# Splitting both halves of a score batch in one slot, and scaling keys and queries on ScalarE instead of VectorE, in a two-layer transformer kernel

## The reference

```
q = (x @ Wq + bq).reshape(b, n, 32, 128)      # k and v alike; b = 1, n = 1024
q = rmsnorm(q, gq);  k = rmsnorm(k, gk)        # over the 128 of a head
scores = einsum('bhnd,bhmd->bhnm', q, k) / sqrt(128)
attn   = softmax(scores)
out    = einsum('bhnm,bmhd->bnhd', attn, v).reshape(b, n, 4096)
return out @ Wo + bo
```

## Time and profile before

| | |
|---|---|
| median of 3 runs | 3506.22 us (3501.73 to 3507.86) |
| the profiled execution | 3506.65 us, of which 3504.5 us lie between its first and last instruction |
| busy over the span | PE 88%, DVE 61%, POOL 45%, ACT 38% |
| TensorE clock granted, mean | 0.96 of full |
| first layer (0 to 1210 us) | PE 1166.98 us busy, clock 0.99 |
| the changed attention (1280 to 3240 us) | PE 1624.39 us busy of 1960, DVE 1331.94, ACT 842.93, POOL 976.06, clock 0.94 |
| last feed-forward part (3240 to 3504 us) | PE 241.71 us busy of 264, clock 0.97 |

### The profile page before, as it was taken

How to read it: one execution, slowest core, us unless ns; L and a number is a source line. 1 busy time by engine, 2 the same in 40 slices (tenths; PEclk the granted TensorE clock), 3 DMA queues, 4 the chain that set the end, 5 groups by cost and what they waited for, 6 DMA issues and landing times. The chain is left out here.

```text
span 3504.5 us, 56557 instructions
## 1 busy us (share of the span) xinstructions
PE 3091.4 (88%) x17632; PEld 2766.9 (79%) x17632; DVE 2131.8 (61%) x3189; ACT 1334.6 (38%) x2375; POOL 1577.9 (45%) x1075
## 2 busy tenths in 40 slices
PE   8999999999999778888888888888888888886998
PEld 7999989898988567777777777777777777775786
DVE  3444444445444576667676666766666676666655
ACT  3333333333333234444444444444444444443322
POOL 3333333333333224544545554554554555444665
PEclk9999999999999999999999999999999999998999
DMA  3211111211121024444454444445444444545642
GB/s 119 59 55 58 54 58 54 59 54 59 53 59 40 22 81 154 159 152 165 153 165 149 158 157 151 161 155 167 150 154 162 149 163 155 163 144 177 179 137 60
DMA packets 311498, 413.82 MB, mean 118 GB/s; under 512 B 35968, under 2 KB 242832, under 8 KB 311312
## 3 DMA queue, kind: packets, MB, share of 16 engines
q1 hardware_dynamic: 273728, 278.05, 27.3%
q10 hardware_dynamic: 37680, 135.02, 9.6%
q0 software_dynamic: 32, 0.02, 0.0%
HBM read 259.85 MB, written 136.31 MB: 113 GB/s over the span
## 5 line engine op out<-in xcount | busy, mean ns | idle before, releaser
L1354 ACT ACTIVATE b_prob<-b_s_ps,b_shift 128x1024 f32<-128x1024 f32 x256 | 286.0, 1117 | 1017.4 <-DVE b_shift L1507 1012.6
L82 PE MATMUL b_pj_kq<-b_w_hi,xT_hi 128*128 128x384 f32 x1008 | 368.3, 365 | 8.4 <-DVE b_nat L1477 8.4
L83 PE MATMUL b_pj_kq<-b_w_lo,xT_hi 128*128 128x384 f32 x1008 | 362.0, 359 | 0.0
L84 PE MATMUL b_pj_kq<-b_w_hi,xT_lo 128*128 128x384 f32 x1008 | 358.1, 355 | 0.0
L1286 POOL TENSOR_TENSOR b_pT_lo<-b_pT_lo,b_pT_hi 128x1024 fp32r<-128x1024 f32 x128 | 303.7, 2373 | 53.1 <-ACT b_pT_hi L1343 53.1
L1286 POOL TENSOR_TENSOR pT_lo<-pT_lo,pT_hi 128x1024 fp32r<-128x1024 f32 x128 | 303.8, 2374 | 48.5 <-ACT pT_hi L1343 48.5
L1513 DVE STREAM_TRANSPOSE b_blocks<-b_prob 128x1024 f32<-128x1024 f32 x256 | 315.5, 1233 | 0.1
L82 PE MATMUL a_pj<-b_w_hi,xT_hi 128*128 128x256 f32 x1024 | 295.4, 288 | 11.9 <-DVE xT_lo L647 11.1
L82 PE MATMUL b_o_ps<-pT_hi,b_v_hi 128*128 128x256 f32 x512 | 159.4, 311 | 165.2 <-POOL pT_lo L1286 165.2
L1507 DVE TENSOR_REDUCE b_shift<-b_s_ps 128x1 f32<-128x1024 f32 x256 | 303.0, 1184 | 0.9 <-PE b_s_ps L84 0.9
L506 ACT ACTIVATE a_sig<-a_pj 128x512 f32<-128x512 f32 x192 | 115.1, 600 | 486.4 <-PE a_pj L84 486.4
(11 more groups left out here) (257 smaller groups left out, 9504.1 us busy)
## 6 DMA issues: line engine op xcount, KB each, us to landing
bounce<-b_blocks ACTq DMA_DIRECT2D x256, 512.0 KB, 2.6
pT_lo<-bounce SPq DMA_DIRECT2D x512, 128.0 KB, 3.0
b_pT_lo<-bounce SPq DMA_DIRECT2D x512, 128.0 KB, 2.8
b_w_raw<-in_w SPq DMA_DIRECT2D x32, 768.0 KB, 4.8
b_w_raw<-in_w SPq DMA_DIRECT2D x95, 256.0 KB, 3.2
a_k_raw<-a_k_blocks SPq DMA_DIRECT2D x512, 32.0 KB, 1.8
a_w_raw<-in_w SPq DMA_DIRECT2D x32, 256.0 KB, 2.7
a_ow_raw<-in_ow SPq DMA_DIRECT2D x32, 256.0 KB, 3.1
```

What stands on the lines that cost most here:

```text
L82: pe.matmul(out, w_hi, x_hi, start=first, stop=False)
L83: pe.matmul(out, w_hi, x_lo, start=False, stop=False)
L84: return pe.matmul(out, w_lo, x_hi, start=False, stop=last)
L1354: act.activation(prob[t % 2][:, :], s_ps[t % 2][:, :], ACT.Exp, bias=shift[:, t:t + 1], accum_out=row_sum[:, t:t + 1]).then_inc(exp_done, 1)
```

## The change

In `split_part`'s place `split_batch` names a whole batch, in even slots alone; ACT and POOL do both halves there, one behind the other. Half 1 moves from the odd slot to the even slot ahead of it, and half 0 stays. `scale_kq` leaves DVE. ACT does it instead, right behind the halves and ahead of the write of the blocks and the exponential, as four copies of 128x128 with a scale (two tiles by keys and queries) in place of one DVE multiplication of 128x512.

```diff
-        def split_part(h, cur, rest, s):
-
-            n = (s - 4) % 8
+        def split_batch(h, cur, rest, s):
+
+            if s % 2:
+                return None
             if s >= 4:
-                return (h, n // 2, n % 2) if cur else None
-            return (h - 1, n // 2, n % 2) if rest else None
+                return (h, (s - 4) // 2) if cur else None
+            return (h - 1, (s + 4) // 2) if rest else None
...
-                    if split_part(h, cur, rest, s):
-                        prob_lo(*split_part(h, cur, rest, s))
+                    if split_batch(h, cur, rest, s):
+                        for part in range(2):
+                            prob_lo(*split_batch(h, cur, rest, s), part)
...
+            def scale_kq(g, bg, i):
+
+                act.wait_ge(rstd_ready, NB * g + i + 1)
+                for u in range(BATCH):
+                    for k in range(2):
+                        part = nat[i][:, u, k * HD:(k + 1) * HD]
+                        last = act.activation(part, part, ACT.Copy, scale=rstd[bg][:, BATCH * i + u, k:k + 1])
+                last.then_inc(kq_scaled, 1)
...
-                    if split_part(h, cur, rest, s):
-                        prob_hi(*split_part(h, cur, rest, s))
+                    if split_batch(h, cur, rest, s):
+                        for part in range(2):
+                            prob_hi(*split_batch(h, cur, rest, s), part)
+                    if nxt and s % 2 == 0:
+                        scale_kq(h + 1, 1 - b, s // 2)
...
-            def scale_kq(g, bg, i):
-                dve.wait_ge(rstd_ready, NB * g + i + 1)
-                both = nat[i][:, :, 0:2 * HD].rearrange("p t (k d) -> p t k d", k=2)
-                dve.tensor_tensor(both, both, rstd[bg][:, BATCH * i:BATCH * (i + 1), :].unsqueeze(3).broadcast_to(
-                    [P, BATCH, 2, HD]), ALU.mult).then_inc(kq_scaled, 1)
...
-                    if nxt and s % 2 == 0:
-                        scale_kq(h + 1, 1 - b, s // 2)
```

## The result

The changed kernel takes 3122.19 us in the median of 4 runs (3120.82 to 3124.98), against 3507.04 us before: a ratio of 0.8906, 95% interval 0.8891 to 0.8922. The profiled execution took 3121.27 us, 3119.4 of them its span. The forecast was 3114.

The account below looks back on a forecast made before the run. A loop through PE's half 1, DVE, ACT and POOL bounds each 15.12 us pair. PE's 11.73 and DVE-ACT's 11.74 tie; plus 0.26 gives 12.0, so 3.12 us over 126 pairs: 3506.65 - 393 = 3114 us, own range 3082 to 3180.

Parts of the forecast that it names:

- The loop that sets the pair: Second layer's attention: PE half 1, projection, DVE, exponential, ACT copies, POOL, PE half 1; 15.12 us a pair of slots.
- PE's floor: PE's own work in a pair of slots at the full clock, never waiting: 11.73 us.
- Four copies on ACT: The four scaled 128x128 key and query copies in the even slot were to take 1.3 us on ACT.
- The spare 0.8 us in front of the even exponential: ACT's copies were to end at 6.35 us, ahead of the even exponential due at 7.13, so hidden.
- The multiplication's price: Moving it off DVE's path between `take` and the exponential was to save the median 1.69 us, of 0.68 to 2.85.
- POOL's spare time: POOL's two halves end near 6.8 and 9.2 us; PE asks at 10.28 and 11.73, 2.5 us to spare.
- The chain of DVE and ACT: From odd exponential to the next odd one through DVE and ACT, weight copies included: 11.74 us a pair.
- The DMAs: The odd tile's block, written and read back, lands at 1.62 us in the next pair; ACT asks at about 2.9.
- the rival of late transfers: If DMAs took twice as long, the loop through memory would set the pair at 14.05 us: 3372 us; chance 8%.
- The 0.26 us for the tie: Estimated addition per pair because two tied loops meeting at four hand-overs don't run at the floor, giving 12.0 us.
- The signs named ahead: PE's wait for low parts under 30 us, clock above 0.98, slot 6.0 us, ACT's wait for DVE's maximum about 1 us.
- The three signs that were to show it wrong: Even exponential waits for nothing (ACT full), PE waits at the transposes, or ACT waits for the reads.

Follow-up runs that it names:

- the split alone: Against the kernel before: both halves made in the even slot, but DVE still multiplies keys and queries at its old place; 3478.47 us, ratio 0.9920.
- the scale alone: Against the kernel before: ACT makes the four scaled copies, but half 1 is still made in the odd slot; 3224.87 us, ratio 0.9195.
- The added wait on POOL: Both halves in the even slot, DVE still multiplying, and POOL's halves made to wait until DVE has multiplied; 3214.26 us, 264 less than without the wait.
- the run with one more sum: Changed kernel with the next head's weights loaded a phase earlier, plus a second sum of squares on DVE per even slot; 3142.86 us, against 3072.18 without it.
- the run without the late block: Changed kernel with the next head's weights loaded a phase earlier, and the bias moved behind the read of tile 1; 3072.18 us, ratio 0.8761.

## Why the prediction was right, point by point

**The loop that sets the pair** was right: with half 1 early and no multiplication 4.1 us of PE's 298 for POOL are left. That both edits are needed is shown by each alone: the split alone ends in the block of DVE, the scale alone leaves the loop closed.

**PE's floor** of 11.73 us was right: 11.69 once nothing else stood in the way.

**Four copies on ACT**, taken at 1.3 us, took 1.27; each lasts 0.389 us and starts about 0.3 after the last. The spare 0.8 us in front of the even exponential was 0.88 in the good pair.

**The multiplication's price**, 1.69 us off DVE as the median of the earlier trace rows, was near what its removal alone gave, 2.04 - 0.47 = 1.57 us. But the prediction did not ask what the spread of 0.68 to 2.85 us was. The trace of before has it:

```profile
2011.53 2.40 POOL L1286 TENSOR_TENSOR pT_lo<-pT_lo,pT_hi 128x1024 fp32r<-128x1024 f32 x1
2012.53 1.95 DVE L1493 TENSOR_TENSOR b_nat<-b_nat,b_rstd 128x512 f32<-128x512 f32 x1
...
2058.41 2.39 POOL L1286 TENSOR_TENSOR b_pT_lo<-b_pT_lo,b_pT_hi 128x1024 fp32r<-128x1024 f32 x1 [0.37 <-ACT b_pT_hi L1343]
2060.70 0.68 DVE L1493 TENSOR_TENSOR b_nat<-b_nat,b_rstd 128x512 f32<-128x512 f32 x1
```

Wherever it starts, it ends about 0.55 us behind POOL's half: 119 of the 128 multiplications start while POOL makes a half, and all of these end 0.54 to 0.63 us behind it. The added wait on POOL shows the cause. For the change itself this made no difference, since the multiplication is gone; for the split alone it is all.

**POOL's spare time**, 2.5 us ahead of PE's half 1, was 1.6 in the good pair: the halves start at 2303.53 and end at 2308.28, and PE starts half 1 at 2309.85. It was enough.

**The chain of DVE and ACT**, 11.74 us, was 0.20 too high if the run with one more sum is read as above: 11.54. Half of that is the weight copies, which start the next instruction after 0.52 us where 0.62 was taken.

**The DMAs** are the step that failed: "Hidden by 1.3 us". The landing of 2.6 us was carried over from the kernel before, where it held for each of a head's eight blocks (2.6 to 2.9 us in the median of each), the last one's 2.63 us included. The prediction did not ask which transfers the shorter pair brings side by side. One block in eight is now written 0.9 us and not 4.0 behind a weight load; there the reads went out 6.65 us after the write, and ACT waited. That is the rival of late transfers, in one pair of four; it costs 12.07 - 11.69 = 0.38 us a pair, or 50 us in all.

**The 0.26 us for the tie** had about the right size for the wrong reason, and that was luck. No such cost shows at this distance of the two loops, since 11.69 us is not above the floor of 11.73; what filled its place was the late block. The forecast came within 8 us with one term too much and one missing. By its own sum without the 0.26 it would have been 3080 us, against 3072 for the run without the late block. The range's upper end of 3180 us goes with 12.5 us a pair only roughly (3177), and 126 pairs were counted where the first and last exponential span 127.5; neither matters here.

**The signs named ahead**: the wait, clock, slot, back-to-back halves, the new copies' 0.39 us and ACT's wait of about 1 us came as said in three pairs of four. The three signs that were to show it wrong all came in the fourth: ACT waited for the reads (31 times, 2.3 us in the mean), PE at the transposes (30 times, 1.5 us), and the even exponential waited for nothing. So the prediction held for the loop and for the number, and not for what was left over in each head.

## What to carry to other kernels

When one instruction shape lasts 0.7 us at one time and 2.9 us at another, look for what runs beside it on the other engine before pricing its removal by the median; here an added wait on POOL gave 264 us. To break a loop, look at every instruction that stands between the releaser and the one that is waited for, on each engine's order, since the loop stays closed as long as one of them is left in it. And ask which transfers a shorter period brings side by side: the write of a head's last block took 2.6 us in the old kernel and over 6 in the new one, with no DMA changed. If two must collide, let it be where the data has a slot to spare.

## What the hardware showed that was not expected

Nearly the same idle time of PE went with two different clocks. With the split alone PE was idle 337 of 1860 us, cut into 332 waits of 1.0 us in the mean, and the granted clock was 1.00. Before, it was idle 308 us of the same 1860, nearly all of it in one wait of 2.4 us in a pair, and the clock was 0.94. With the scale alone one wait of 1.06 us stood at the same place in a pair, and the clock was 1.00; the pair became 2.2 us shorter, though only 1.6 us of DVE had left the loop. No run changed the length of a wait and nothing else, so this is seen, not shown.

The stretch before, and with the split alone:

```profile
1290.00:3150.00 1860.00, 1552.33 (x8433) 1412.32 (x8434) 1269.09 (x1811) 802.75 (x1449) 932.84 (x605) 0.94 0.48 157
```
```profile
1290.00:3150.00 1860.00, 1523.17 (x8557) 1309.95 (x8558) 1450.30 (x1841) 806.26 (x1475) 1001.49 (x613) 1.00 0.48 159
```

And the waits of PE with the split alone, 1290 to 3150 us:

```profile
PE b_y_ps L82 <- DVE x_nat L1546: 152.6, 119, 1.3
...
PE b_pj_kq L1421 <- DVE b_nat L1505: 122.4, 121, 4.9
...
PE b_pj_kq L82 <- DVE b_nat L1489: 61.9, 92, 3.9
```
